# Deformable sampling on one Trainium2 core: four gather buffers, a pair of index words ahead, and three of four corners weighted by small multiply-adds

## The chip, the cores and the metric

The kernel runs on one core of one Trainium2 chip, in float32 throughout. The metric is the device time of one execution in microseconds (us); lower is better. The chip's engines are named as the profile names them: PE (TensorE, matmuls), DVE (VectorE), ACT (ScalarE), POOL (GpSimd) and SP (SyncE, which here only issues loads).

## The reference

`x` is (8, 256, 128, 128). Layer 0 normalizes it by groups, predicts offsets and a modulation with a 3x3 convolution, samples a 1x1-convolved `v` bilinearly at the offset positions, and adds a 1x1 convolution of the result to `x`. Layer 1 is a group-wise ZCA whitening of the whole batch.

```python
x = x + _L0_conv_ref(_gn(x), ...)      # per image, layer 0
    offsets = conv2d(x, offset_w, offset_b, 1)          # 2*4 channels
    mod = 1.0 + jnp.tanh(conv2d(x, mod_w, mod_b, 1))    # 4 channels
    v = conv2d(x, kv_w, kv_b, 0)[:, C:].reshape(B, HEADS, HD, H, W)
    # _sample_one: four corners of each position
    return g(x0, y0, w00) + g(x1, y0, w01) + g(x0, y1, w10) + g(x1, y1, w11)
    sampled = _sample(v, grid) * mod
    out = conv2d(sampled.reshape(B, C, H, W), out_w, out_b, 0)
x = x + _L1_conv_ref(_gn(x), ...)      # needs the covariance over all images
```

The sampling is what the change touches: for every pixel and each of 4 channel groups, 4 corners of 64 channels are fetched and summed with 4 weights (modulation folded in).

## The kernel before, in words

**Stages.** The program first takes the statistics of image 0, then runs a software pipeline over images: while image g is sampled (its `v` gathered from DRAM), image a = g + 1 goes through the convolution that makes its `v` and its offsets, and image s = g + 2 gives its statistics. Image g = 7 is sampled alone, and image 6 without a third one beside it. After the last image the whitening matrices are computed, and a last phase (L1074, L780) streams all data once through a 128x128 map.

**Tiling.** An image is 16 pairs of two blocks of 4 rows. Index `i` is the pair, `j` the block in it. For one block, POOL issues 16 indirect DMAs (`gather`, L829), one for each of 4 rows x 4 groups; each brings, for 128 pixels (partitions), a patch of 256 floats, the four corners of 64 channels. `NJ` = 16, and the half `h` holds 8 of them. So a pair has 32 gathers and 4 halves.

**Order on each engine.** Every engine runs its own program in order, with semaphores between them. For one block (i, j) in the pipeline's middle:
- DVE: `sample` of half 0 (wait for its gathers; L568 multiplies all corners by their weights, L570 and L573 add them up into `samp`), `residual` (L582) of the block before, `conv_out` (L483, L486) of rows 0 and 1 of image a, `sample` of half 1, `take_stats` (L418), `conv_out` of rows 2 and 3, and after j = 1 `place` (L510 to L555), which makes indices and weights of a pair of image a.
- PE: convolution rows 0, 1 (L929), `out_conv` of the block before (L965), `turn_x1` of it (L979, needs `residual`), row 2, after j = 1 `offsets` (L941), `turn_samples` of half 0 (L954), row 3, `turn_samples` of half 1, and `gram_block` (L994) of the block before.
- ACT: store and copy-out of the block before (`x1_store` L1116, `x1_out` L1126, needs `turn_x1`), `dup` of rows 0, 1 (L1092, L1094, needs `conv_out`), `samples_out` (L1109, needs `turn_samples` of half 1), `indices` (L1140, the index words of block (i + 1, j)), `dup` of rows 2, 3, `v_store` (L1100), and after j = 1 the tanh of the modulation (L1145).
- POOL: `gather`, which waits until `sample` of (i - 1, j) has read the patch buffer, and for the index words.
- SP: loads of x for the three images.

There are two patch buffers, one for each j. The pair loop (`pairs`, L227) runs pair 0 apart, pairs 1 to 14 in a hardware loop with one pair in its body, and pair 15 apart; for the six middle images a loop over images (L222) stands around it. At the last pair of an image DVE, PE and ACT also run `prep`, the normalization of the next image's weights (L444 to L467).

Of the kernel before, what the change touches and what calls it, by code (L numbers as in the profile page):

```python
# [5 lines left out]
ALU = mybir.AluOpType  # L25
# [27 lines left out]
NH = NJ // 2  # L53
S0 = 4 * BP
# [25 lines left out]
def deform_zca_kernel(nc, B, x, wA, biasA, bias_off, wO, bias_o, w_z, bias_z, out):  # L80
# [10 lines left out]
    with ctx:  # L91
# [28 lines left out]
        taps = sb("taps", [P, H + 2, NT])  # L120
# [3 lines left out]
        xa = [sb(f"xa{j}", [P, CC, BP]) for j in range(2)]  # L124
        vring = [sb(f"vring{j}", [P, ROWS, G, 2, CG]) for j in range(2)]
        carry = [sb(f"carry{j}", [P, G, CG]) for j in range(2)]
        index_now = [sb(f"index_now{j}", [P, NJ], U32) for j in range(2)]
        patch = [sb(f"patch{j}", [P, NJ, PATCH]) for j in range(2)]
# [7 lines left out]
        xs = [sb(f"xs{j}", [P, CC, BP]) for j in range(2)]  # L136
# [6 lines left out]
        pm = {n: sb("p_" + n, [P, QR, G]) for n in ("tm", "th", "w0", "w1", "ia")}  # L143

# [33 lines left out]
        got = [[sem(f"got{j}{h}") for h in range(2)] for j in range(2)]  # L178
        weighted = sem("weighted")
        halved = sem("halved")  # L180
# [65 lines left out]
        def offsets_use(b, q, more):  # L246


            if ends(q)[1]:
# [5 lines left out]
               for j in range(2)]  # L255
# [31 lines left out]
        y_mem = taps[:, :, :].rearrange("p r n -> p (r n)")  # L287
        y_buf = [area(y_mem, n * CC * YB, CC * YB).rearrange("p (c n) -> p c n", c=CC)
                 for n in range(NY - 2)]
# [16 lines left out]
        def _(eng):  # L306
# [9 lines left out]
            def load_s(b, i, j):  # L316

                at = eng.snap((i * 2 + j) * BP)
                p = eng.snap((b - 1) * PAIRS + i)
                eng.wait_ge(st_used[j], p + 1)  # L320
                alone(eng)
                eng.dma_start(xs[j][:, :, :], x_v[bass.ds(b, 1), :, :, bass.ds(at, BP)]
                              .rearrange("a p c n -> (a p) c n")).then_inc(st_ld[j], 16)

            def load_a(b, i, j):
# [5 lines left out]
                eng.dma_start(xa[j][:, :, :], x_v[bass.ds(b, 1), :, :, bass.ds(at, BP)]  # L331
# [13 lines left out]
            def image(g, a, s):  # L345
# [10 lines left out]
                def pair(i):  # L356
# [40 lines left out]
        def _(eng):  # L397
            for row in (0, H + 1):
                eng.memset(taps[:, row, :], 0.0).then_inc(setup_v, 1)
# [7 lines left out]
            eng.wait_ge(setup_v, 6)  # L407
# [5 lines left out]
            eng.wait_ge(setup_v, 8)  # L413
# [57 lines left out]
            def conv_out(b, i, j, rows, wide):  # L471

                for r in rows:
                    k = r % 2
# [3 lines left out]
                    if r == ROWS - 1:  # L478
# [7 lines left out]
                    eng.tensor_tensor(taps[:, bass.ds((i * 2 + j) * ROWS + r + 1, 1), :]  # L486
                                      .rearrange("p a n -> p (a n)"),
                                      bank[:, C:NA], biasB[:, C:NA], ALU.add)\
# [72 lines left out]
            def sample(b, i, j, h):  # L561

                eng.wait_ge(got[j][h], (b * PAIRS + i) * (NH * 16) + NH * 16)
                mine = patch[j][:, h * NH:(h + 1) * NH, :]
                v4 = mine.rearrange("p t (k e) -> p (t k) e", e=CG)
                w4 = weight[:, bass.ds(((i * 2 + j) * 2 + h) * (NH * 4), NH * 4)].unsqueeze(2)\
                    .to_broadcast([P, NH * 4, CG])
                eng.tensor_tensor(v4, v4, w4, ALU.mult).then_inc(weighted, 1)  # L568
                eng.wait_ge(weighted, (b * PAIRS + i) * 4 + 2 * j + h + 1)
                eng.tensor_tensor(mine[:, :, 0:ENT], mine[:, :, 0:ENT], mine[:, :, ENT:PATCH],  # L570
                                  ALU.add).then_inc(halved, 1)
                eng.wait_ge(halved, (b * PAIRS + i) * 4 + 2 * j + h + 1)
                eng.tensor_tensor(samp[j][:, 2 * h:2 * h + 2, :].rearrange("p r (g e) -> p (r g) e", g=G),  # L573
# [678 lines left out]
```

## Time and profile before

| what | value |
|---|---|
| median of 3 runs | 6903.72 us (6898.48 to 6908.78) |
| span of the profiled execution | 7542.0 us (its own time; nothing is recorded outside the span) |
| PE / DVE / ACT / POOL busy | 61% / 56% / 14% / 61% |
| mean granted TensorE clock | 0.806 |
| DMA | 1612.36 MB, mean 214 GB/s |

The profiled execution is 638 us longer than the median run. Shares of busy time are means over stages: the gathers run from 289.6 to about 6806 us of the span, and the last phase from about 6906 us to the end is bound by DMA.

### The profile page before, as it was taken

To read this page: it belongs to the slowest core of one execution; us is meant where nothing else is said; L and a number is where in the kernel's file an instruction comes from. 1 tells how busy PE (TensorE), PEld (TensorE's weight loads), DVE (VectorE), ACT (ScalarE), POOL (GpSimd) and SP (SyncE) were. 2 spreads that over 40 slices of the span, in tenths; PEclk is the share of its full clock that TensorE was granted. 3 is DMA by queue.
4 is the path that set the end of the run, shared out by engine and by line. 5 is a ranking of instruction groups with operands and counts; after the bars stand their busy time and mean duration, and the time that the engine had idled before them with its cause. 6 is when DMAs were issued, how large, how long until landed. Compare 5 with 4: busy or idle time off the path is not lost.

```text
span 7542.0 us, 73500 instructions
## 1 busy us (share of the span) xinstructions
PE 4572.0 (61%) x17916; PEld 2935.6 (39%) x17916; DVE 4223.0 (56%) x8110; ACT 1067.2 (14%) x2723; POOL 4578.9 (61%) x4115
## 2 busy tenths in 40 slices
PE   5765656565566656655665656566665544446777
PEld 3443434344344433333443434343443333234322
DVE  6655656555565555555655556555555544345555
ACT  1211111111111111111111111111111111010000
POOL 0377667676767767667676677676776777770000
PEclk9877778787788878777887878787887766667999
DMA  8866657666666666666666666565565544445999
GB/s 283 275 203 212 200 185 227 195 205 201 197 206 207 209 194 208 197 193 207 202 216 196 201 206 217 188 216 186 184 195 183 187 131 136 129 129 193 421 421 412
DMA packets 1069670, 1612.36 MB, mean 214 GB/s; under 512 B 92080, under 2 KB 617008, under 8 KB 1067568
## 3 DMA queue, kind: packets, MB, share of 16 engines
q0 software_dynamic: 196608, 537.13, 22.2%
q10 hardware_dynamic: 632832, 536.91, 22.0%
q1 hardware_dynamic: 240176, 537.77, 20.7%
q14 instruction: 42, 0.34, 0.0%
q8 instruction: 12, 0.20, 0.0%
HBM read 1074.58 MB, written 536.87 MB: 214 GB/s over the span
## 4 chain that ended last, share of the span: by engine, by line
another core or an unknown queue 21%; issue 21%; PE 19%; DVE 18%; DMA 9%; POOL 5%; DVEq 3%; ACT 3%; ACTq 1%; POOLq 0%; SPq 0%
PE psA L929 6%; DVE patch L568 5%; PE psO L965 5%; POOL patch L829 5%; DMA out_dram<-vring 4%; DVE patch L570 4%; PE psG L994 3%; DMA vring<-x 3%; PE psT L954 2%; DVE xr L582 2%; DMA v<-vring 1%; DVE vring L483 1%; PE psT L979 1%; DVE bst L418 1%
## 5 line engine op out<-in xcount | busy, mean ns | idle before, releaser
L829 POOL DMA_INDIRECT patch<-v,index_now x4096 | 4572.9, 1116 | 2224.0 <-issue 1517.0
L568 DVE TENSOR_TENSOR patch<-patch,weight 128x2048 f32<-128x2048 f32 x512 | 1171.3, 2288 | 941.4 <-DMA patch<-v,index_now 553.1
L929 PE MATMUL psA<-wB,xa 128*128 128x364 f32 x3824 | 1498.5, 529 | 185.2 <-DVE taps L486 103.1
L979 PE MATMUL psT<-ident,xr 128*128 128x128 f32 x2048 | 373.8, 343 | 1712.3 <-issue 928.5
L582 DVE SCALAR_TENSOR_TENSOR xr<-psO,bo_sb,xr 128x512 f32<-128x512 f32 x512 | 375.2, 748 | 1205.9 <-remote 972.5
L979 PEld LDWEIGHTS psT<-ident,xr 128*128 128x128 f32 x2048 | 300.6, 177 | 1917.7 <-issue 1067.8
L965 PE MATMUL psO<-sampT,wO_sb 128*128 128x512 f32 x2048 | 985.3, 626 | 73.4 <-issue 42.1
L929 PEld LDWEIGHTS psA<-wB,xa 128*128 128x128 f32 x3824 | 769.6, 218 | 574.4 <-issue 208.8
L954 PE MATMUL psT<-ident,samp 128*128 128x128 f32 x2048 | 409.9, 329 | 674.2 <-DVE samp L573 440.1
L1126 ACT ACTIVATE x1T<-psT 128x512 f32<-128x512 f32 x512 | 290.0, 596 | 3629.8 <-PE psT L979 1597.1
L994 PE MATMUL psG<-x1T 128*128 128x129 f32 x4096 | 664.6, 329 | 29.8 <-issue 18.7
L994 PEld LDWEIGHTS psG<-x1T 128*128 128x128 f32 x4096 | 643.7, 246 | 30.9 <-issue 27.1
L570 DVE TENSOR_TENSOR patch<-patch 128x1024 f32<-128x1024 f32 x512 | 627.2, 1225 | 17.6
L954 PEld LDWEIGHTS psT<-ident,samp 128*128 128x128 f32 x2048 | 289.7, 170 | 877.0 <-DVE samp L573 510.9
L965 PEld LDWEIGHTS psO<-sampT,wO_sb 128*128 128x128 f32 x2048 | 410.4, 204 | 543.5 <-issue 503.1
L1109 ACT ACTIVATE sampT<-psT 128x512 f32<-128x512 f32 x512 | 283.7, 595 | 1684.3 <-remote 711.5
L483 DVE TENSOR_TENSOR vring<-psA,biasB 128x256 f32<-128x256 f32 x734 | 303.4, 413 | 185.2 <-remote 114.7
L573 DVE TENSOR_TENSOR samp<-patch 128x512 f32<-128x512 f32 x512 | 354.2, 692 | 17.6
L1094 ACT ACTIVATE vring<-vring 128x256 f32<-128x256 f32 x768 | 290.7, 412 | 54.3 <-DVE vring L483 49.1
L941 PEld LDWEIGHTS psI<-taps,shift 128*128 128x128 f32 x2304 | 279.2, 193 | 31.2 <-issue 3.2
L418 DVE BATCH_NORM_STATS2 bst<-xs 128x512 f32 (+1 forms) x448 | 285.8, 680 | 3.9 <-DMA xs<-x_dram 3.9
L483 DVE TENSOR_TENSOR carry<-psA,biasB 128x256 f32<-128x256 f32 x222 | 92.8, 418 | 341.3 <-remote 295.6
(176 smaller groups left out, 2935.5 us busy)
## 6 DMA issues: line engine op xcount, KB each, us to landing
v<-vring ACTq DMA_DIRECT2D x256, 1024.0 KB
xa<-x_dram SPq DMA_DIRECT2D x256, 512.0 KB
xr<-x_dram SPq DMA_DIRECT2D x256, 512.0 KB
x<-xr ACTq DMA_DIRECT2D x256, 512.0 KB
xs<-x_dram SPq DMA_DIRECT2D x224, 512.0 KB
taps<-x SPq DMA_DIRECT2D x96, 1024.0 KB, 13.4
out_dram<-taps ACTq DMA_DIRECT2D x96, 1024.0 KB, 18.9
patch<-v,index_now POOLq DMA_INDIRECT x4096
```

The costliest lines, as they stand in the source:

```text
L418: ins = eng.bn_stats(bst[:, c, bass.ds(i * 2 + j, 1), :] .rearrange("p a s -> p (a s)"), xs[j][:, c, :])
L483: eng.tensor_tensor(dst, bank[:, 0:C].rearrange("p (g e) -> p g e", g=G), biasB[:, 0:C].rearrange("p (g e) -> p g e", g=G), ALU.add)\
L568: eng.tensor_tensor(v4, v4, w4, ALU.mult).then_inc(weighted, 1)
L570: eng.tensor_tensor(mine[:, :, 0:ENT], mine[:, :, 0:ENT], mine[:, :, ENT:PATCH], ALU.add).then_inc(halved, 1)
L573: eng.tensor_tensor(samp[j][:, 2 * h:2 * h + 2, :].rearrange("p r (g e) -> p (r g) e", g=G), mine[:, :, 0:CG], mine[:, :, CG:ENT], ALU.add)\
L582: eng.scalar_tensor_tensor(xr[j][:, o, :], psO[o][:, :], bo_sb[:, o:o + 1], xr[j][:, o, :], ALU.add, ALU.add)\
L829: eng.indirect_dma_start(out=patch[j][:, t, :], out_offset=None, in_=v2_flat[k], in_offset=bass.IndirectOffsetOnAxis(ap=index_now[j][:, t: ...
L929: mm = eng.matmul(conv_bank[wide][r][:, 0:NA], xa[j][:, c, r * W:(r + 1) * W], wB[:, c, :], start=(c == 0), stop=(c == CC - 1))
L954: mm = eng.transpose(psT[c][:, r * W:(r + 1) * W], samp[j][:, r, c * P:(c + 1) * P], ident[:, :])
L965: mm = eng.matmul(psO[o][:, :], wO_sb[:, h, o * P:(o + 1) * P], sampT[:, h, :], start=(h == 0), stop=(h == CC - 1))
L979: mm = eng.transpose(psT[h][:, at:at + P], xr[j][:, c, row * W:(row + 1) * W], ident[:, :])
L994: mm = eng.matmul(psG[:, c * (P + 1):(c + 1) * (P + 1)], x1T[:, r, c, 0:P], x1T[:, r, c, :], start=(opens and c == 0 and r == 0), stop=(cl ...
```

## The change

It has four parts.
- **Four patch buffers** (`RING` = 4) instead of two. The pair loop now has two pairs in its body, so that pair parity `m` picks buffer `2 * m + j` by name. A gather waits for the samples of two pairs before, not one.
- **Index words a pair ahead**: ACT copies them, and now also 64 weights per block (`weight_now`), before it does anything else for the block, instead of after `samples_out`.
- **Taps in strips**: the tap rows of image a, kept for a whole image before, live in two strips of 10 rows. The rows at a strip's edge are written twice. The buffers of the last phase move to other memory.
- **The weighting**: corner 0 of each gather is scaled by ACT in place (128x64, weight read per partition), corners 1 to 3 are multiplied and added by DVE, one 128x64 instruction for each corner and gather.

```diff
-            pair(0)
-            with eng.Fori(1, PAIRS - 1) as i:
-                pair(i)
-            pair(PAIRS - 1)
+            pair(0, 0, 0)
+            with eng.Fori(0, PAIRS // 2 - 1) as h:
+                pair(eng.snap(h * 2 + 1), 1, h)
+                pair(eng.snap(h * 2 + 2), 0, eng.snap(h + 1))
+            pair(PAIRS - 1, 1, PAIRS // 2 - 1)
...
-            def sample(b, i, j, h):
-
-                eng.wait_ge(got[j][h], (b * PAIRS + i) * (NH * 16) + NH * 16)
...
-                eng.tensor_tensor(v4, v4, w4, ALU.mult).then_inc(weighted, 1)
...
+            def sample(b, i, m, j, h):
+
+                n = 2 * m + j
+                half = (b * PAIRS + i) * 4 + 2 * j + h
+                eng.wait_ge(scaled, half + 1)
+                if h == 0:
+                    eng.wait_ge(psT_free[CC - 1], (b * PAIRS + i) * 4 + 2 * j + SAMP_FREE - 3)
+                for k in (1, 2, 3):
+                    for t in range(h * NH, (h + 1) * NH):
+                        total = patch[n][:, t, 0:CG]
+                        r, at = t // G, t % G * CG
+                        last = eng.scalar_tensor_tensor(
+                            samp[j][:, r, at:at + CG] if k == 3 else total,
+                            patch[n][:, t, k * CG:(k + 1) * CG],
+                            weight_now[n][:, t * 4 + k:t * 4 + k + 1], total, ALU.mult, ALU.add)
+                    if k < 3:
+                        last.then_inc(weighted, 1)
+                        eng.wait_ge(weighted, half * 2 + k)
+                    else:
+                        last.then_inc(sampled[j][h], 1)
...
+            def scale(b, i, m, q, j, h):
+
+                n = 2 * m + j
+                eng.wait_ge(index_cp, (b * PAIRS + i) * 2 + j + 1)
+                eng.wait_ge(got[n][h], (b * (PAIRS // 2) + q) * (NH * 16) + NH * 16)
+                for t in range(h * NH, (h + 1) * NH):
+                    corner = patch[n][:, t, 0:CG]
+                    last = eng.activation(corner, corner, ACT.Copy,
+                                          scale=weight_now[n][:, t * 4:t * 4 + 1])
+                last.then_inc(scaled, 1)
...
                     for j in range(2):
+                        if not last:
+                            if g is not None:
+                                indices(g, i + 1, 1 - m, j)
+                        elif a is not None:
+                            indices(a, 0, 0, j)
                         if g is not None:
+                            scale(g, i, m, q, j, 0)
                             if j == 1:
                                 x1_store(g, i, 0)
                                 x1_out(g, i, 0)
@@ -1161,12 +1197,8 @@
                         if ca is not None and not (prepare and j == 0):
                             dup(ca, ci, j, (0, 1))
                         if g is not None:
+                            scale(g, i, m, q, j, 1)
                             samples_out(g, i, j)
-                        if not last:
-                            if g is not None:
-                                indices(g, i + 1, j)
-                        elif a is not None:
-                            indices(a, 0, j)
```

On DVE, in the pair loop, the instructions of one half and its neighbours stood like this before (`ISA` and `REGISTER_ALU` are register steps):

```order
L568 ISA
L568 TENSOR_TENSOR patch<-patch,weight 128x2048
L569 REGISTER_ALU
L570 TENSOR_TENSOR patch<-patch 128x8x128
L573 TENSOR_TENSOR samp<-patch 128x512
L418 ISA
L418 BN_STATS bst<-xs 128x6
```

And with the change, at the same place:

```order
L562 REGISTER_ALU
L569 SCALAR_TENSOR_TENSOR patch<-patch,weight_now 128x64 x8
L575 ISA
L569 SCALAR_TENSOR_TENSOR patch<-patch,weight_now 128x64 x8
L575 REGISTER_ALU
L569 SCALAR_TENSOR_TENSOR samp<-patch,weight_now 128x64 x8
L407 ISA
L407 BN_STATS bst<-xs_mem 128x6
```

Three instructions have become 24, in three rounds of 8 with a wait between the rounds.

On ACT, block j = 1 of the pair loop before, from the copy-out of the block before to the next block (`x<-xr` is `x1_store`):

```order
L1116 DMA x<-xr 128x2x512
L1123 REGISTER_ALU
L1125 REGISTER_ALU
L1126 ACTIVATE x1T<-psT 128x4x128 x2
L1090 REGISTER_ALU
L1092 ACTIVATE vring<-carry 128x4x64
L1094 ACTIVATE vring<-vring 128x4x64
L1090 REGISTER_ALU
L1094 ACTIVATE vring<-vring 128x4x64
L1108 REGISTER_ALU
L1109 ACTIVATE sampT<-psT 128x512 x2
L1140 ACTIVATE index_now<-index 128x16
```

With the change, for one block:

```order
L1159 ACTIVATE index_now<-index 128x16
L1165 ISA
L1166 ISA
L1169 ACTIVATE patch<-patch,weight_now 128x64 x8
L1131 REGISTER_ALU
L1132 ISA
L1132 DMA x<-xr 128x2x512
L1139 REGISTER_ALU
L1141 REGISTER_ALU
L1142 ACTIVATE x1T<-psT 128x4x128 x2
L1106 ISA
L1108 ACTIVATE vring<-carry 128x4x64
```

The index words have moved from behind `samples_out` to the front, and eight scalings stand ahead of `x1_store` and `x1_out`; the other eight stand between `dup` of rows 0, 1 and `samples_out`.

At the end of `place` DVE's pair loop before branches back after each pair (the last two of four stores of `weight`, then the branch):

```order
L555 ISA
L555 SCALAR_TENSOR_TENSOR weight<-p_m,p_w 128x32
L555 ISA
L555 SCALAR_TENSOR_TENSOR weight<-p_m,p_w 128x32
L557 REGISTER_ALU
L230 REGISTER_ALU
L230 COMPARE_AND_BRANCH
```

With the change the first pair of the body runs on into the second, and only the second ends with a branch back:

```order
L552 SCALAR_TENSOR_TENSOR weight<-p_m,p_w 128x32
L554 REGISTER_ALU
L562 ISA
L569 SCALAR_TENSOR_TENSOR patch<-patch,weight_now 128x64 x8
L575 ISA
```

Counted in the built programs, with register steps and waits, one pass of DVE's pair loop in the middle images has 114 instructions before and 390 after; one pass of the loop over images around it had 322 before, without repeating the pair loop. ACT's pair loop goes from 58 to 193.

## Rows read from the trace of the kernel before

**Rows 1.** Busy time by window, the gathers' stretch; its first row names the columns.

```profile
core 0: us, PE busy (x) PEld busy (x) DVE busy (x) ACT busy (x) POOL busy (x), PEclk, DMA share, GB/s
289.60:6813.00 6523.40, 3833.10 (x15847) 2566.99 (x15848) 3618.92 (x6699) 995.32 (x2535) 4572.94 (x4096) 0.78 0.61 193
```

**Rows 2.** The page, part 5, gathers: busy us, mean ns of one, idle before.

```profile
L829 POOL DMA_INDIRECT patch<-v,index_now x4096 | 4572.9, 1116 | 2224.0 <-issue 1517.0
```

**Rows 3.** Waits of POOL: us in total, times, longest us.

```profile
POOL patch L829 <- ACT index_now L1140: 707.0, 105, 15.9
```

**Rows 4.** Timeline 2999:3006, POOL and DVE: start us, us, instruction, [idle before].

```profile
3000.45 0.94 POOL L829 DMA_INDIRECT patch<-v,index_now  x1 [0.30 <-issue]
3001.49 2.29 DVE L568 TENSOR_TENSOR patch<-patch,weight 128x2048 f32<-128x2048 f32 x1 [5.03 <-DMA patch<-v,index_now]
3001.70 2.90 POOL L829 DMA_INDIRECT patch<-v,index_now  x1 [0.30 <-issue]
3003.81 1.23 DVE L570 TENSOR_TENSOR patch<-patch 128x1024 f32<-128x1024 f32 x1
```

**Rows 5.** Timeline 3140:3185, one block whose patches had all landed.

```profile
3154.84 2.29 DVE L568 TENSOR_TENSOR patch<-patch,weight 128x2048 f32<-128x2048 f32 x1 [0.78 <-DVE weight L555]
3159.03 1.40 DVE L582 SCALAR_TENSOR_TENSOR xr<-psO,bo_sb,xr 128x512 f32<-128x512 f32 x2
3161.32 1.09 ACT L1126 ACTIVATE x1T<-psT 128x512 f32<-128x512 f32 x2 [8.55 <-PE psT L979]
3162.59 0.72 ACT L1094 ACTIVATE vring<-vring 128x256 f32<-128x256 f32 x2
3165.27 0.69 DVE L573 TENSOR_TENSOR samp<-patch 128x512 f32<-128x512 f32 x1
3168.09 2.28 DVE L568 TENSOR_TENSOR patch<-patch,weight 128x2048 f32<-128x2048 f32 x1
3168.60 0.38 ACTq L1100 DMA_DIRECT2D v<-vring  x1
```

**Rows 6.** Timeline 3140:3185, `place` and small operations beside it.

```profile
3150.57 0.18 DVE L510 TENSOR_TENSOR p_tm<-psI,off_b 128x32 f32<-128x32 f32 x1
3150.98 0.22 ACT L1140 ACTIVATE index_now<-index 128x16 uint32 x1
3151.08 0.42 ACT L1094 ACTIVATE vring<-vring 128x256 f32<-128x256 f32 x1
3152.49 0.22 DVE L540 SCALAR_TENSOR_TENSOR p_m<-p_ix,p_b 128x64 f32<-128x64 f32 x1
3152.64 0.22 DVE L542 TENSOR_TENSOR p_m<-p_ix,p_c 128x64 f32<-128x64 f32 x1
```

**Rows 7.** Timeline 7010:7016, DVE in the last phase.

```profile
7011.95 1.41 DVE L780 SCALAR_TENSOR_TENSOR vring<-psT,patch,vring 128x512 f32<-128x512 f32 x2 [2.26 <-PE psG L1074]
7013.27 0.74 DVE L780 SCALAR_TENSOR_TENSOR vring<-psI,patch,vring 128x512 f32<-128x512 f32 x1
```

**Rows 8.** Timelines 3140:3185 and 3000:3056, PE's `out_conv` at two clocks.

```profile
3170.75 3.60 PE L965 MATMUL psO<-sampT,wO_sb 128*128 128x512 f32 x8
...
3038.34 6.39 PE L965 MATMUL psO<-sampT,wO_sb 128*128 128x512 f32 x8 [3.56 <-issue]
```

**Rows 9.** Timeline 1924:1977, DVE from image to image.

```profile
1926.67 2.28 DVE L568 TENSOR_TENSOR patch<-patch,weight 128x2048 f32<-128x2048 f32 x1
1950.84 2.28 DVE L568 TENSOR_TENSOR patch<-patch,weight 128x2048 f32<-128x2048 f32 x1
...
1967.55 0.52 DVE L555 SCALAR_TENSOR_TENSOR weight<-p_m,p_w 128x32 f32<-128x32 f32 x4
1969.64 0.41 DVE L591 TENSOR_TENSOR gram<-gram,psG 128x258 f32 x1
1976.07 2.29 DVE L568 TENSOR_TENSOR patch<-patch,weight 128x2048 f32<-128x2048 f32 x1 [6.01 <-issue]
```

**Rows 10.** The page, part 3, the queue of instruction packets.

```profile
q14 instruction: 42, 0.34, 0.0%
```

More of the change, by code:

```diff
@@ L134, in deform_zca_kernel @@
         gram_tail = sb("gram_tail", [P, B, CC, P + 1])
-        xs = [sb(f"xs{j}", [P, CC, BP]) for j in range(2)]
+        xs_mem = sb("xs_mem", [P, 2, CC, BP])
         bst = sb("bst", [P, CC, BLOCKS, 6])
@@ L143, in deform_zca_kernel @@
         pm = {n: sb("p_" + n, [P, QR, G]) for n in ("tm", "th", "w0", "w1", "ia")}
+        xa = [xa_mem[:, j, :, :] for j in range(2)]
+        xs = [xs_mem[:, j, :, :] for j in range(2)]
         psA = [ps(f"psA{i}") for i in range(2)]
@@ L177, in deform_zca_kernel @@
         index_cp = sem("index_cp")
-        got = [[sem(f"got{j}{h}") for h in range(2)] for j in range(2)]
+        got = [[sem(f"got{n}{h}") for h in range(2)] for n in range(RING)]
+        scaled = sem("scaled")
+        edge = sem("edge")
         weighted = sem("weighted")
-        halved = sem("halved")
         sampled = [[sem(f"sampled{j}{h}") for h in range(2)] for j in range(2)]
@@ L397, in _ @@
         def _(eng):
-            for row in (0, H + 1):
-                eng.memset(taps[:, row, :], 0.0).then_inc(setup_v, 1)
+            eng.memset(taps[:, 0, 0, :], 0.0).then_inc(setup_v, 1)
             eng.memset(x1T[:, :, :, :], 1.0).then_inc(setup_v, 1)
@@ L469, in prep, with conv_out @@
                 eng.wait_ge(psI_free, b * NU + 3)
-            def conv_out(b, i, j, rows, wide):
+            def conv_out(b, i, m, j, rows, wide):
+                top = ends(i)[0]
                 for r in rows:
-                    k = r % 2
+                    k, row = r % 2, j * ROWS + r
                     eng.wait_ge(row_full[j][r], b * PAIRS + i + 2)
@@ L610, in pair @@
                     prepare = last and ca is not None
+                    if last and a is not None and s is None:
+                        eng.memset(taps[:, m, QR + 1, :], 0.0).then_inc(edge, 1)
                     for j in range(2):
                         if g is not None:
-                            sample(g, i, j, 0)
+                            sample(g, i, m, j, 0)
                             if j == 1:
@@ L839, in _ @@
                     alone(eng)
-                    with eng.Fori(0, PAIRS) as i:
-                        for j in range(2):
-                            gather(b, k, i, j)
+                    with eng.Fori(0, PAIRS // 2) as q:
+                        for m in range(2):
+                            for j in range(2):
+                                gather(b, k, q * 2 + m, m, j)
         def whiten_tensor(eng):
@@ L931, in conv_rows, with offsets @@
                     mm.then_inc(row_full[j][r], 1)
-            def offsets(b, q, more):
+            def offsets(b, q, m, more):
+                bottom = ends(q)[1] and not more
                 for k in range(2):
-                    eng.wait_ge(psA_free[k], (b * PAIRS + q) * 4 + 5 + (0 if ends(q)[1] else 2))
+                    eng.wait_ge(psA_free[k], (b * PAIRS + q) * 4 + (5 if bottom else 7))
+                if bottom:
+                    eng.wait_ge(edge, 1)
                 eng.wait_ge(psI_free, offsets_use(b, q, more))
```

115 lines of the change are left out of this document (63 added, 52 removed).

## The prediction

> **What bounds the kernel now.** I read the windows first. The gathers fill 6523 us of the 7542 us span [rows 1]; what lies around them, 1019 us, is statistics, the first convolution, the whitening and a DMA-bound last phase, which the change leaves alone but for the places of some buffers. The gathers are 4096 = 128 pairs of 32, and they last 1116 ns in the mean with about 0.30 us between two [rows 2, 4]. So POOL needs 32 x (1.116 + 0.305) = 45.5 us for a pair. The profiled execution spends 51 us on a pair, but it is 638 us longer than the median run. If the 1019 us are the same in both, an undisturbed run spends (6904 - 1019) / 128 = 45.98 us on a pair: within half a microsecond of what POOL needs with no wait at all. In an undisturbed run POOL is the bound, and its waits for the index words (707 us in the profile, [rows 3]) have mostly gone. I therefore work in time per pair and apply the difference to the median.
>
> Second, why a gather takes 1.116. Undisturbed it takes 0.94; the one that starts at 3001.70 takes 2.90, and ends 0.82 us after DVE's 2.29 us multiply L568 [rows 4]. It waits until the big two-input instruction is over, and then it gets through although L570, again with two inputs, has already begun. There are four L568 a pair, and (1.116 - 0.949) x 32 = 5.3 us a pair is their price. 0.949 is what I take for a free gather, from 0.94 to 0.95 in the timelines.
>
> Third, how fast the other engines could go. At 3154.84 all patches had landed, and the next block's first L568 follows 13.25 us later [rows 5]. With the 4.3 us of `place` in every second block [rows 6] that is about 31 us a pair, far under POOL's 45.5. DVE, PE and ACT are waiting for POOL now.
>
> **POOL after the change.** No instruction of 2.29 us is left in the gathers' way. If the small ones hand over between two of them, as L568 does to the gather ahead of L570 [rows 4], each gather loses at most part of one small instruction, and POOL needs 32 x (0.949 + 0.305) = 40.1, say 40.5 us. If DVE kept POOL out through all 24, POOL would need about 48; the handover row speaks against it. Buffers and early index words remove waits of which, by the sum above, an undisturbed run has half a microsecond a pair. So POOL offers 5.5 us a pair. Whether they are taken depends on the others.
>
> **One DVE multiply-add, d.** A 64-column two-input instruction without a pointer starts 0.15 us before the next [rows 6]; that is the low end. The weight here is read per partition. L780 is such an instruction: two take 1.41 us and one 0.74, so the second starts 0.67 after the first [rows 7]. A column costs (2.29 - 1.23) / 1024 = 1.035 ns [rows 4], 0.53 for 512, so 0.14 is fixed; with 64 columns d = 0.20. The high end is no overlap at all, 0.74 - 0.53 + 0.07 = 0.28. I take 0.20, the nearest row. A half becomes 24d + 0.3 (two waits between rounds, and the tail) = 5.1 us, where before L568 to the end of `sample` is 2.32 + 1.26 + 0.69 = 4.2.
>
> **One ACT scaling, a.** No row shows an activation with a pointer. Without one, 16 columns are followed after 0.10 us [rows 6] and 256 after 0.31 (the pair in 0.72, [rows 5]): 0.14 for 64 columns, the low end. Without overlap 0.22 + 48 x 0.0009 = 0.26, the high end. DVE's pointer costs 0.05 (0.15 to 0.20), which would give 0.19; I take 0.23, between that and the high end. Eight take 8a + 0.1 = 1.9 us, and DVE can't begin before the last one is done.
>
> The Trainium skill, ScalarE: Activation LUTs, section What ACT_TABLE_LOAD costs, gives 186 ns + 0.833 ns a column, 93 ns for each pointer operand, and 93 ns of overlap. By it a would be 0.24 (an estimate from that page), and the sum below 25 to 30 us higher; no run here has shown it yet.
>
> **The chain of a block.** With POOL out of the way the in-order chain is what sets the time, and ACT now stands in it. From the block of [rows 5]:
> - scalings of half 0, 8a + 0.1; its sample, 24d + 0.3; `residual`, 1.4.
> - from its end (3160.43) PE turns x1, ACT copies it out and does `dup` of rows 0, 1, until 3163.31: 2.9 us, of which the next ACT instruction can take back 0.1. Before, `sample` of half 1 went on beside this. Now its scalings are queued behind it.
> - scalings of half 1, 8a + 0.1; its sample, 24d + 0.3.
> - from its end (3165.96) to the issue of the v store (3168.98) ACT has 3.0 us, then 0.25 of index and weight words, before the next block's scalings.
>
> Sum for j = 0: 16a + 48d + 8.25. After j = 1 DVE has `take_stats` and rows 2, 3 (2.4 us with the doubled tap row) and then `place`, 4.3 us from 3150.57 to 3154.84; the scalings hide behind them: 8a + 48d + 11.5. A pair is 24a + 96d + 19.75 = 5.5 + 19.2 + 19.75 = 44.5 us. It was 31 before; it is now over POOL's 40.5.
>
> PE adds a little. From the end of `sample` of half 1 (3165.96) PE reaches the end of `out_conv` at 3174.35, 8.4 us, with the clock at its upper level [rows 5, 8]; the next `residual` needs it after 3.25 + 1.9 + 5.1 = 10.3 us. At the lower level `out_conv` alone takes 6.4 instead of 3.6 [rows 8], and is late by 0.9. The granted clock is 0.78 in this stretch [rows 1], and PE now idles longer inside a block. I add 0.5 us a pair, bounds 0 and 1.2.
>
> **The loop body.** In the loop over images DVE's way back, over 322 instructions, costs it a stop: the last store of `weight` ends at 1968.07, and the next image's first L568 starts at 1976.07, with only `residual` and `gram_add` in between and 6.01 us idle on "issue" [rows 9]. At the pair loop's way back (114 instructions) the same place takes 0.78 us [rows 5]. The difference is an instruction fetch, about 6.8 us. The changed pair loop has 390 instructions on DVE, more than the 322 that had to be fetched again. So I expect the stop at each of the 7 passes an image: 6.8 x 7 / 16 = 3.0 us a pair. It falls right behind `place`, where the chain runs on DVE. Bounds: nothing if the body stays resident, twice that if a second stop comes.
>
> The Trainium skill, Runtime: NRT & Kernel Launch, section Instruction fetch mechanics, says that a taken branch to a page that isn't in the current window of two forces a fetch and a stall; the 6.01 us of [rows 9] agrees. It also puts 512 instructions into that memory, by which 390 fit if they lie in two pages; then this term is nothing, which is the first rival below.
>
> **Image ends.** With POOL waiting anyway, `prep` was hidden. From the L568 at 1926.67 to the one at 1950.84 is 24.2 us [rows 9], where two halves take 13.25 [rows 5]; of the 17.6 more I count 14, since PE has less behind it afterwards, six times.
>
> **Sum.** Images 0 to 5: 16 x (44.5 + 0.5 + 3.0) + 14 = 782 each, 4692. Image 6, without statistics, 1.2 less a pair: 749. Image 7 has no convolution, `dup` or `place`; its chain is about 39, under POOL: 16 x 40.5 = 648. Together 6089, against 128 x 45.98 = 5885: 204 us more, 6904 + 204 = 7108, which I round to **7105 us**. DMA moves the same bytes at a share of 0.61 [rows 1] and isn't a bound at 48 us a pair.
>
> **Rivals.**
> - *The loop stays resident.* Then 48 us go in each of seven images: 6775. For it: the ratio of 390 to 322 says little if pages' edges decide.
> - *POOL stays the bound.* With d = 0.14 and a = 0.14 the chain is 36.6, and with the stop 39.6: POOL sets 40.5, the time is 6904 - 128 x 5.5 = 6200. It needs the pointer to cost nothing on either engine; L780 speaks against it. The chain decides from 40.5 us on, which is d = 0.12 with the stop and a = 0.23.
> - *Small instructions don't overlap on DVE* (d = 0.28): 7.7 us more in 112 pairs and 6 in the last 16, 8065. L780's overlap of 0.07 speaks against it.
> - *The stop comes twice a pass*: 7105 + 7 x 48 = 7440.
> - *Costs cancel*: the chain at 45.98 with a short stop; nothing measurable, within 0.2%, 14 us, which is what a measurement of this kernel tells from no change.
>
> **How the numbers follow.** My forecast 0.53, resident loop 0.20, POOL 0.10, twice 0.07, no overlap 0.05, cancel 0.05. The likeliest case's own range is 6950 to 7280: d by 0.01 is 110 us, a by 0.03 80, the clock 80. To leave out no more than 2 in 10 the range goes from 6700, below the resident loop's 6775, to 7350. Faster: POOL 0.10, most of the resident loop 0.17, a corner of the forecast 0.03: 0.30. Same 0.05. Slower 0.65.
>
> **What the changed profile would show.** Gathers of more than 1 us nearly gone, and POOL waiting for index words or samples instead; DVE's 128x64 instructions 0.20 us apart, ACT's 0.23; DVE idle in front of half 1's first multiply-add until ACT's scaling; an idle of some 6 us on "issue" behind every second `place`, and several hundred instruction packets where there are 42 now [rows 10]. I am wrong if pairs run at 40 us with POOL never waiting, or if the packets stay few.

## The result, and the profile after

| | median | runs |
|---|---|---|
| before | 6901.1 us | 6886.09 to 6908.78, 4 |
| changed | 7044.98 us | 7034.64 to 7056.14, 4 |

The ratio is 1.0209, 95% interval 1.0194 to 1.0223: the change makes the kernel 2.1% slower. The forecast was 7105. The profiled execution of the changed kernel took 7052.57 us, its span is 7050.8, so its stretches can be read against the median directly.

From the page, changed kernel: busy time, the instruction queue, the chain that ended last, and three groups (busy us, mean ns, idle before):

```profile
PE 4741.2 (67%) x17916; PEld 3135.5 (44%) x17916; DVE 4642.1 (66%) x19126; ACT 2116.8 (30%) x7075; POOL 3934.5 (56%) x4115
...
q14 instruction: 302, 2.47, 0.1%
...
DVE 45%; ACT 19%; issue 14%; PE 9%; DMA 8%; ACTq 2%; DVEq 1%; SPq 0%
...
L838 POOL DMA_INDIRECT patch<-v,index_now x4096 | 3928.6, 959 | 2366.6 <-issue 1557.5
L569 DVE SCALAR_TENSOR_TENSOR patch<-patch,weight_now 128x64 f32<-128x64 f32 x8192 | 1701.3, 280 | 1838.2 <-ACT patch L1169 1530.8
...
L1169 ACT ACTIVATE patch<-patch,weight_now 128x64 f32<-128x64 f32 x4096 | 1030.0, 336 | 0.5
```

The gathers are nearly free now, 959 ns where [rows 2] has 1116, and they keep POOL busy 644 us less (3928.6 against 4572.9). The chain that ended last holds no POOL: it is DVE and ACT, and DVE waits 1531 us for ACT's scaling.

The timeline of two blocks, DVE (a pair starts at 2977.39, the next at 3022.63, its second block at 3044.45):

```profile
2970.45 0.60 DVE L552 SCALAR_TENSOR_TENSOR weight<-p_m,p_w 128x32 f32 x4
2977.39 1.26 DVE L569 SCALAR_TENSOR_TENSOR patch<-patch,weight_now 128x64 f32<-128x64 f32 x6 [6.34 <-issue]
...
3022.63 3.35 DVE L569 SCALAR_TENSOR_TENSOR patch<-patch,weight_now 128x64 f32<-128x64 f32 x16 [0.34 <-DVE weight L552]
3026.01 1.66 DVE L569 SCALAR_TENSOR_TENSOR samp<-patch,weight_now 128x64 f32<-128x64 f32 x8
3027.58 1.41 DVE L584 SCALAR_TENSOR_TENSOR xr<-psO,bo_sb,xr 128x512 f32<-128x512 f32 x2
...
3033.86 3.35 DVE L569 SCALAR_TENSOR_TENSOR patch<-patch,weight_now 128x64 f32<-128x64 f32 x16 [3.36 <-ACT patch L1169]
3037.25 1.66 DVE L569 SCALAR_TENSOR_TENSOR samp<-patch,weight_now 128x64 f32<-128x64 f32 x8
...
3044.45 3.35 DVE L569 SCALAR_TENSOR_TENSOR patch<-patch,weight_now 128x64 f32<-128x64 f32 x16 [3.35 <-ACT patch L1169]
...
3073.51 1.67 DVE L569 SCALAR_TENSOR_TENSOR patch<-patch,weight_now 128x64 f32<-128x64 f32 x8 [7.15 <-issue]
```

And ACT in the first of them:

```profile
3029.93 1.08 ACT L1142 ACTIVATE x1T<-psT 128x512 f32<-128x512 f32 x2 [7.85 <-PE psT L992]
3030.90 0.42 ACT L1108 ACTIVATE vring<-carry 128x256 f32<-128x256 f32 x1
3031.21 0.72 ACT L1110 ACTIVATE vring<-vring 128x256 f32<-128x256 f32 x2
3031.82 2.01 ACT L1169 ACTIVATE patch<-patch,weight_now 128x64 f32<-128x64 f32 x8
```

Two things can be read from these rows. Half 1 can't start at 3030.5, when DVE is through with rows 0 and 1, but waits 3.36 us: its scalings are queued on ACT behind x1's copy-out, which waits for PE, which waits for `residual`. And the pair that begins behind the loop's way back (2970.45 to 2977.39, 3067 to 3073.51) has 6.3 and 7.2 us idle on "issue", where the same place inside the body (3022.63) has 0.34. Over all 42 such ways back the idle time before the pair is 4.8 to 7.6 us, 6.6 in the median.

Measured from the first L569 of a pair to the next, a pair takes 45.2 us without the way back and 50.5 with it (medians of images 0 to 5); an image 771 to 776 us, of which the last pair has 65 to 69; image 6 732; a pair of image 7 39.5. In image 7 POOL gathers nearly without a pause, a pair in 40.6, yet it doesn't hold DVE up: from its second pair on DVE reaches a half 11 to 26 us after the half's last gather, and waits there for nothing but ACT's scalings. It works off a stock of patches at its own pace.

### The profile page after: what moved, and what is told of

It reads as the page before. It is cut to its first block, busy times and chain, and to the rows that moved or that the text cites. A ratio compares the mean times of both kernels' runs of the same rounds, so it can differ in the third digit from the quotient of the medians.

```text
span 7050.8 us, 87497 instructions
## 1 busy us (share of the span) xinstructions
PE 4741.2 (67%) x17916; PEld 3135.5 (44%) x17916; DVE 4642.1 (66%) x19126; ACT 2116.8 (30%) x7075; POOL 3934.5 (56%) x4115
## 3 DMA queue, kind: packets, MB, share of 16 engines
q10 hardware_dynamic: 632832, 536.91, 22.5%
## 4 chain that ended last, share of the span: by engine, by line
DVE 45%; ACT 19%; issue 14%; PE 9%; DMA 8%; ACTq 2%; DVEq 1%; SPq 0%
DVE patch L569 22%; ACT patch L1169 11%; DVE samp L569 10%; DMA out_dram<-vring 4%; DVE xr L584 3%; ACT vring L1110 3%; PE psT L992 3%; DMA vring<-x 3%; DVE bst L407 2%; PE psT L967 1%; ACT x1T L1142 1%; DMA v<-vring 1%; ACT sampT L1125 1%; ACT vring L1108 1%; PE psA L939 1%
## 5 line engine op out<-in xcount | busy, mean ns | idle before, releaser
L838 POOL DMA_INDIRECT patch<-v,index_now x4096 | 3928.6, 959 | 2366.6 <-issue 1557.5
L569 DVE SCALAR_TENSOR_TENSOR patch<-patch,weight_now 128x64 f32<-128x64 f32 x8192 | 1701.3, 280 | 1838.2 <-ACT patch L1169 1530.8
L939 PE MATMUL psA<-wB,xa_mem 128*128 128x364 f32 x3824 | 1502.6, 533 | 93.5 <-DVE taps L485 86.8
L1169 ACT ACTIVATE patch<-patch,weight_now 128x64 f32<-128x64 f32 x4096 | 1030.0, 336 | 0.5
L939 PEld LDWEIGHTS psA<-wB,xa_mem 128*128 128x128 f32 x3824 | 799.4, 226 | 482.8 <-issue 136.3
L569 DVE SCALAR_TENSOR_TENSOR samp<-patch,weight_now 128x64 f32<-128x64 f32 x4096 | 849.6, 280 | 18.2
L1007 PE MATMUL psG<-x1T 128*128 128x129 f32 x4096 | 855.6, 396 | 7.7 <-ACT x1T L1142 7.7
L1007 PEld LDWEIGHTS psG<-x1T 128*128 128x128 f32 x4096 | 835.3, 311 | 9.5 <-issue 7.1
L407 DVE BATCH_NORM_STATS2 bst<-xs_mem 128x512 f32 (+1 forms) x448 | 285.9, 681 | 3.9 <-DMA xs_mem<-x_dram 3.9
L954 PE MATMUL psI<-taps,shift 128*128 128x96 f32 x2304 | 279.6, 277 | 0.0
```

What stands on the lines that cost most here:

```text
L407: ins = eng.bn_stats(bst[:, c, bass.ds(i * 2 + j, 1), :] .rearrange("p a s -> p (a s)"), xs[j][:, c, :])
L569: last = eng.scalar_tensor_tensor(samp[j][:, r, at:at + CG] if k == 3 else total, patch[n][:, t, k * CG:(k + 1) * CG], weight_now[n][:, t ...
L838: eng.indirect_dma_start(out=patch[n][:, t, :], out_offset=None, in_=v2_flat[k], in_offset=bass.IndirectOffsetOnAxis(ap=index_now[n][:, t: ...
L939: mm = eng.matmul(conv_bank[wide][r][:, 0:NA], xa[j][:, c, r * W:(r + 1) * W], wB[:, c, :], start=(c == 0), stop=(c == CC - 1))
L954: mm = eng.matmul(psI[:, 0:QR * NO].rearrange("p (r o) -> p r o", o=NO), shift[:, dx, :], taps[:, m, dy:dy + QR, t * NO:(t + 1) * NO], sta ...
L1007: mm = eng.matmul(psG[:, c * (P + 1):(c + 1) * (P + 1)], x1T[:, r, c, 0:P], x1T[:, r, c, :], start=(opens and c == 0 and r == 0), stop=(cl ...
```

## The experiments

**First, a thing that most of them met.** In four of the six sets of runs below the kernel before took 7471 to 7635 us, not 6900. Their traces show why: a semaphore update often arrives microseconds after the instruction that makes it. Timeline of the changed kernel in a run of that kind (after_again), PE and DVE:

```profile
3029.19 1.39 PE L939 MATMUL psA<-wB,xa_mem 128*128 128x364 f32 x4
3031.11 1.66 DVE L569 SCALAR_TENSOR_TENSOR samp<-patch,weight_now 128x64 f32<-128x64 f32 x8
3032.68 0.42 DVE L473 TENSOR_TENSOR vring<-psA,biasB 128x256 f32<-128x256 f32 x1
...
3036.49 1.11 PE L967 MATMUL psT<-ident,samp 128*128 128x128 f32 x4 [5.91 <-remote]
...
3038.22 0.42 DVE L473 TENSOR_TENSOR carry<-psA,biasB 128x256 f32<-128x256 f32 x1 [4.95 <-remote]
```

The sample that PE turns at 3036.49 was finished at 3032.77, and the row that DVE takes at 3038.22 had left PE at 3030.6; the semaphore events that end these two waits stand at 3036.45 and 3038.11. Counted from the semaphore events of each trace, the table gives the share of PE's, DVE's and ACT's updates that came over 0.3 us late, for those made while POOL gathers (a burst is the 16 gathers of a block) and for all others:

```
trace           while POOL gathers  else    mean gather us  burst of 16 us  between bursts us
changed kernel  0.001               0.000   0.959           19.9            2.1
before          0.348               0.020   1.116           22.5            0.3
r_big           0.347               0.016   1.113           22.3            0.3
b_piece4        0.448               0.018   0.984           20.3            4.4
r_piece4        0.482               0.025   0.980           20.3            6.3
b_new2          0.467               0.029   0.958           19.9            10.2
after_again     0.558               0.030   0.960           20.0            7.1
a_straight      0.566               0.038   0.960           19.9            7.0
a_pace          0.002               0.000   0.966           22.1            1.1
a_fs_again      0.003               0.000   0.962           20.0            0.3
```

The shares are soft. The traces with late updates record only 69 to 80% of the updates of PE, DVE and ACT, and 12 to 24% of those of the gathers, where the others record 98% or more. With every update that finds no record counted as late, the share is 0.49 for before and 0.65 for after_again; with those left out that find none within 15 us, 0.35 and 0.54. It stays under 0.005 for the changed kernel, a_pace and a_fs_again either way. The time is no matter of counting: with late updates the kernel before takes 8 to 11% longer, the changed kernel 17%.

So the trace of before, from which I predicted, was one with late updates, and its time (7542 us) lies among those of the kernel before in the late sets; that accounts for the 638 us over its median. It is no trait of one chip: after_again (late) and a_fs_again (prompt) ran on the same one. I call the runs late and prompt; each ratio is to the kernel before, run beside it on the same chip.

**r_big** (late): the changed kernel with the old weighting.

```diff
-                        last = eng.scalar_tensor_tensor(   # 24 a half
...
+                            last = eng.tensor_tensor(v4, v4, w4, ALU.mult)   # 128x2048, then two additions
...
-                            scale(g, i, m, q, j, 0)   # and half 1: nothing is scaled on ACT
```

> The changed kernel (four patch buffers, index words a pair ahead, taps in strips, pair loop of two pairs) with the old weighting: three wide DVE instructions a half, nothing scaled on ACT. Theory A (the new weighting's chain through ACT and DVE costs the time, and POOL was the bound before): gathers are held back again, mean 1.10 to 1.12 us, POOL 45.5 us a pair with hardly a wait, so 128 x 45.5 + 1050 = 6870, within 0.5% of before; the loop body of some 300 DVE instructions may still stop at its way back, but POOL has buffers ahead and hides it. Theory B (the four-buffer structure with its long loop body is what slows the kernel): 7000 or more, with DVE's stops on the chain. Rival C (before, POOL really lost more to late index words than half a microsecond a pair): 6750 or less.

Measured: 1.0145 (1.003 to 1.0259; it rests on two runs, 7522 and 7541 us, since the other two took 7649 and 14676). Gathers:

```profile
L847 POOL DMA_INDIRECT patch<-v,index_now x4096 | 4556.8, 1113 | 2219.5 <-issue 1551.6
```

The slow gathers are back, as theory A has it, and bursts follow each other after 0.3 us. With late updates B is out: the structure costs 1.5% here, not 10 like the whole change (after_again). No run has this kernel with prompt updates, so the 6870 of A and the 6750 of C stay untested.

**b_new, b_new2** (late, on two chips): the new weighting alone in the kernel before.

```diff
+scale(g, i, j, 0)   # ACT, ahead of x1_store / x1_out
+scale(g, i, j, 1)   # ACT, ahead of samples_out
```

> The kernel before (two buffers, loop of one pair, index words after the block) with the new weighting alone: corner 0 on ACT, 24 multiply-adds a half on DVE. Theory A: the chain of a pair is 45.2 us, as between two stops in the changed kernel, but the loop of some 210 DVE instructions stays resident and has no stop: images 0 to 5 are 16 x 45.2 + 21 = 744, image 6 713, image 7 about 660, with 1020 around them 6860: 0 to 1% faster than before, some 180 faster than the changed kernel. Theory B (the new weighting in itself costs the 2%, whatever the loop): 7040 or more. If two buffers make POOL late as well, pairs are at 47 or more, POOL idle on index words, and 7100 or more.

> The same kernel as b_new (the new weighting alone in the kernel before). Its loop over pairs, 201 instructions on DVE, came back in 0.3 us each time in b_new. Where updates are prompt, theory A expects pairs at 45 to 46 us, no stop, 6860 with bounds 6800 and 6960; theory B (the new weighting costs the 2% whatever the loop) 7040 or more; if two buffers make POOL late, 7100 or more. If updates are late again, as b_new, 15% over the kernel before.

Measured: 1.1499 (1.1421 to 1.1577) and 1.1763 (1.1681 to 1.1845). The way back of the pair loop (201 instructions) took DVE 0.2 to 0.5 us every time. My time was missed by far; POOL was idle 7.4 (b_new) and 10.2 us (b_new2) between bursts in the median, in all 2423 and 2638 us for index words. That with two buffers late signals also stop POOL fits this, but wasn't tested by itself. What the weighting costs alone with prompt updates stays open.

**b_piece4** (late): the old weighting in pieces of 512 columns.

```diff
-eng.tensor_tensor(v4, v4, w4, ALU.mult)                 # 128x2048
+for q0 in range(0, NH, NH // parts): ... eng.tensor_tensor(...)   # parts 4, 2, 1; all 128x512
```

> The kernel before with its wide weighting cut into pieces of 512 columns: four multiplies, two additions, one addition a half, all on DVE, nothing else changed. Theory A (a gather waits for the end of the one DVE instruction with two inputs that it meets, so its length is the price): gathers of 2.9 us are gone, none loses more than about 0.6, the mean falls from 1.116 to about 1.0, POOL needs 41 to 42 us a pair; two buffers and late index words may leave it waiting a little; 6330 to 6550. Rival (DVE keeps POOL out for its whole two-input work, however it is cut): mean stays at 1.10 or more, time within 1% of before or slower, since the pieces add some 0.3 us a half.

Measured: 1.0116 (1.0053 to 1.0178); gathers

```profile
L841 POOL DMA_INDIRECT patch<-v,index_now x4096 | 4029.6, 984 | 2805.1 <-issue 1529.0
```

The mechanism of [rows 4] is confirmed: the same columns in shorter instructions take 132 of the 167 ns off a gather. The 543 us that POOL saves went into the pauses between bursts, 4.4 us in the median instead of 0.3. **r_piece4** (late), the same in the changed kernel:

> The changed kernel (four buffers, early index words, loop of two pairs, 258 instructions on DVE) with the weighting in wide pieces on DVE and nothing on ACT: four multiplies, two additions, one addition of 512 columns a half. It takes both costs away at once: no 2.29 us instruction ahead of POOL, no ACT link and no stop at the way back (226 instructions came back in 0.3 to 0.7 in r_big). Gathers at a mean of 0.98 as in b_piece4. Where updates are prompt, theory A: POOL needs 32 x (0.98 + 0.305) = 41.1 us a pair, DVE's chain 32 to 34, so 128 x 41.1 + 1050 = 6310, bounds 6250 and 6450. Rival (something else than POOL and the ACT link set the pairs): 6800 or more. Where updates are late, POOL's burst of 20.5 us and what follows it stand in a row: 51 us a pair, 7450 to 7600, about the kernel before.

Measured 1.057 (1.0502 to 1.0637), above the range that I gave for late updates: 6.3 us between bursts.

**a_actfirst, a_first2** (late, two chips): ACT's order.

```diff
 scale(g, i, m, q, j, 0)
+scale(g, i, m, q, j, 1)
 x1_store(...); x1_out(...); dup(...)
-scale(g, i, m, q, j, 1)
 samples_out(g, i, j)
```

> The changed kernel with ACT's order changed in one place: the eight scalings of half 1 follow those of half 0 at once, ahead of x1_store, x1_out and dup. Theory A (half 1 waits 3.3 us a block because its scalings are queued behind x1_out and dup): DVE's idle before the half-1 multiply-adds goes from 3.3 to 3.8 us to nearly 0, a pair from 45.2 to about 39, then POOL's 39.5 to 40.5 is the bound; the stops stay but are mostly covered by patches fetched ahead; 6300 to 6450. Rival (PE is right behind ACT: the idle only moves to residual, which waits for out_conv): pairs at 43 or more, 6800 to 7000. Rival (the scalings take a share of something DVE needs): DVE's multiply-adds get longer than 0.20 apart.

> The same kernel as a_actfirst (all sixteen scalings of a block ahead of ACT's other work), run again because in the four runs so far a third of the semaphore updates came microseconds after the instruction that made them, where in the changed kernel's trace all but 7 come within 0.02 us, and the kernel before took 7471 us beside them, not 6901. Where updates are prompt, theory A expects DVE's wait ahead of half 1 gone, pairs at 39 to 41 us with POOL as the bound, 6300 to 6450. Rival (the idle moves to PE's out_conv and turns): pairs at 43 or more, 6800 or more. If updates are late again, the run is as a_actfirst, about 9% over the kernel before.

Measured: 1.0923 (1.0857 to 1.0989) and 1.0918 (1.0846 to 1.0991). DVE's idle ahead of half 1 went from 3.8 us (after_again) to nothing in the median, as expected, and the time hardly moved: pairs still alternate between 60 and 50 us as in after_again below, and DVE is idle 189 us an image until an update that the trace puts down to "remote", where after_again has 74 (means of images 1 to 5).

**a_straight and after_again** (late, side by side): DVE's program written out.

```diff
+if eng is nc.vector:
+    for i in range(PAIRS):
+        pair(i, i % 2, i // 2)
+    return
 pair(0, 0, 0)
 with eng.Fori(0, PAIRS // 2 - 1) as h:
```

> The changed kernel with DVE's program alone written out for all 16 pairs of an image instead of a loop of two pairs; every other engine keeps its loop, and no operation is added or left out. Theory A (the way back over 390, or 370, instructions stops DVE for 5 to 6 us, six times in each of seven images, and nothing covers it): every pair of images 0 to 5 takes 45.2 us, the 50.5 us pairs are gone, 42 x 5.3 = 220 us less where updates are prompt: 6825, 1.1% under the kernel before. Straight code has no taken branch, so instructions arrive ahead. Rival (the 5.3 us are no fetch but work at the seam of the loop, or code that runs straight is fetched as late): pairs alternate 45.2 and 50.5 as before, 7045. If updates are late again the idle after place goes too, but less of the time, since late updates set the pairs.

> The changed kernel itself, beside the kernel before on this chip. If updates are prompt: ratio 1.021 as before. If they are late: theory A (each signal between ACT, DVE and PE costs more there, and the changed kernel has more of them in a row in a block) 1.08 to 1.12, pairs at 53 to 60 us; rival (late updates cost both kernels the same time) 1.02.

Measured: a_straight 1.0928 (1.0866 to 1.0991), the changed kernel 1.0997 (1.0936 to 1.1058). Pairs of image 0 are, in us:

```
after_again  53.8 54.2 60.0 49.8 59.9 49.3 60.0 49.8 60.1 50.5 60.1 50.4 60.2 51.2 54.3 72.3
a_straight   53.4 54.2 54.8 54.1 54.8 53.3 54.8 54.1 54.8 53.4 54.8 53.6 54.1 53.4 54.2 72.6
```

The 60 and 50 (a stop, and the pair after it catching up) become 54: the stop belongs to the taken branch; between the pairs of straight code it is gone, though instructions are fetched there too (221 packets against 303). a_fs_again below shows it with prompt updates: between its pairs DVE has no idle time on "issue" at all. The loop over images still branches back, over 2929 instructions, and there DVE still stops, 2.7 to 5.0 us here and 4.9 to 6.2 in a_fs_again. The intervals of the two ratios overlap; by one trace of each, an image of 0 to 5 takes 887.0 instead of 899.5 us in the mean, 2.1 us a stop, since the next pair catches up with most of it where updates are late.

**a_pace** (prompt): POOL slowed down.

```diff
     ).then_inc(got[n][t // NH], 16)
+    eng.memset(idle[:, t, :], 0.0).then_inc(paced, 1)      # 128x192, after every gather
```

> The changed kernel with a small write of POOL's own (192 columns of a scratch tile) behind every gather, and nothing else changed: POOL gathers more slowly, a gather every 1.5 to 1.6 us instead of 1.25. Theory L (where updates are late, the chip hands on only some 11 of them a microsecond; every gather makes 16, so 16 in a burst of 20 us are 12.8 a microsecond, a backlog builds up behind which the signals of PE, DVE and ACT wait, and it has gone some 3 us after the burst; the kernel before, whose gathers DVE holds up, makes 11.3): at 10 to 10.7 a microsecond there is no backlog, the share of updates that are late while POOL gathers falls from 0.56 to under 0.2, the 7 us between two bursts shrink to 1 or less, a pair is 49 to 52 us instead of 54 to 55: 7450 to 7750, that is 0.99 to 1.03 of the kernel before instead of 1.10, though POOL does more. Rival (updates are late whenever POOL gathers, at any pace): share still 0.5, bursts of 24.5 and 7 between them, 63 us a pair, 9000. Where updates are prompt: POOL at 49 to 51 becomes the bound, 7350 to 7550.

Measured: 7174.46 us, 1.0391 (1.0374 to 1.0408). Timeline, POOL:

```profile
5899.40 0.95 POOL L842 DMA_INDIRECT patch<-v,index_now  x1 [0.17 <-issue]
5900.35 0.27 POOL L846 MEMSET idle<- 128x192 f32 x1
5900.79 0.95 POOL L842 DMA_INDIRECT patch<-v,index_now  x1 [0.17 <-issue]
```

A gather every 1.39 us, not my 1.5 to 1.6, so 7350 was too high. It ran with prompt updates, so theory L (a limit of some 11 updates a microsecond) is untested. But it is the cleanest test of what bounds the changed kernel. POOL now needs 46.4 us a pair instead of 40.6. A pair of image 7 goes from 39.5 to 46.2 us, 87 us over 15 pairs: there POOL has become the bound, and DVE reaches a half 4 to 5 us after its last gather. An image of 0 to 5 goes from 772.7 to 778.8 in the mean, 0.4 us a pair, though POOL needs 5.8 more: there it isn't the bound.

**a_first_straight** (late) and **a_fs_again** (prompt): the same kernel twice, ACT's order and DVE's straight code together.

> The changed kernel with ACT's sixteen scalings at the start of the block and DVE's program written out, both edits of the runs before together. Where updates are prompt, theory A: chain 45.2 - 6.7 = 38.5 us a pair and no stop, POOL's 39.5 to 40.5 sets the pairs, 6200 to 6300, 10% under the kernel before. Rival (PE's out_conv or the turns take the idle's place): 6600 or more. Where updates are late, DVE's waits come from the updates that the burst of gathers holds back, and the two edits take 0.6% each or less: 8080 to 8170, 8 to 9% over the kernel before.

> The same kernel as a_first_straight (scalings of both halves at the start of the block, DVE's program written out), run again since the chips differ and one with prompt updates can tell the theories apart by time. Where updates are prompt, theory A: chain 45.2 - 6.7 = 38.5 us a pair and no stop, POOL's 39.5 to 40.5 sets the pairs; 128 x 40.2 + 6 x 10 for the ends of images + 1050 = 6250, bounds 6150 and 6450, some 9% under the kernel before. Rival (PE's out_conv or the turns take the place of the idle time): pairs at 43 or more, 6600 or more. Where updates are late, as a_first_straight: 1.06 to 1.09 of the kernel before, pairs at 54.

Measured: late 1.0688 (1.0641 to 1.0735). Prompt: **6226.34 us** (6222.82 to 6239.29) against 6917.1, ratio 0.8999 (0.8986 to 0.9011), where 6250 was expected. From its page, the chain and the gathers, and DVE in one block:

```profile
q14 instruction: 221, 1.81, 0.1%
...
POOL 50%; issue 19%; DMA 10%; DVE 8%; PE 8%; ACT 3%; ACTq 1%; POOLq 0%; DVEq 0%; SPq 0%
...
L842 POOL DMA_INDIRECT patch<-v,index_now x4096 | 3940.8, 962 | 1546.3 <-issue 1538.6
```

```profile
3001.00 3.36 DVE L573 SCALAR_TENSOR_TENSOR patch<-patch,weight_now 128x64 f32<-128x64 f32 x16 [3.36 <-ACT patch L1173]
3004.40 1.66 DVE L573 SCALAR_TENSOR_TENSOR samp<-patch,weight_now 128x64 f32<-128x64 f32 x8
3005.97 1.41 DVE L588 SCALAR_TENSOR_TENSOR xr<-psO,bo_sb,xr 128x512 f32<-128x512 f32 x2
...
3008.30 3.39 DVE L573 SCALAR_TENSOR_TENSOR patch<-patch,weight_now 128x64 f32<-128x64 f32 x16
3011.73 1.66 DVE L573 SCALAR_TENSOR_TENSOR samp<-patch,weight_now 128x64 f32<-128x64 f32 x8
```

Half 1 starts 7.30 us after half 0 instead of 11.23, with no wait. POOL now waits for nothing: its 1546.3 us before gathers are 4095 times 0.305 and the 297 before the first one, against 2366.6 in the changed kernel; DVE reaches a half 4 us after its last gather in image 7, so here POOL is the bound. Images 0 to 5 take 652 us in the mean instead of 773, image 6 632 instead of 732. The same operations and bytes, 12% less time than the changed kernel.

## Why the prediction was right

Slower was right, by 144 us instead of 204. By its steps:

- **POOL before and after.** The price of L568 is confirmed by r_big (1113 ns) and b_piece4 (984); the gathers came to 959 instead of 949, and a POOL that hardly waits needs 40.4 to 40.6 us a pair (a_fs_again, and image 7 of the changed kernel), forecast 40.1 to 40.5. That the kernel before was bound by POOL with prompt updates rests on the arithmetic from its median; no prompt trace of it was taken, so it is argued, not shown.
- **d and a.** From start to start, DVE's multiply-adds lie 0.20 us apart (eight in 1.66, the last one 0.28; a half takes 5.04, forecast 5.1), forecast 0.20. ACT's eight in 2.01 with 0.336 for the last give a = 0.239, forecast 0.23. The prices that the Trainium skill gives in ScalarE: Activation LUTs, section What ACT_TABLE_LOAD costs (186 ns + 0.833 a column, 93 for a pointer operand, 93 of overlap), come to an estimate of 0.24 for it, and the trace agrees.
- **The chain of a block.** Forecast 44.5 + 0.5 us (the terms for j = 1 add to 11.6, not 11.5), measured 45.2. The wait where it was said to be: 3.36 us in front of half 1, for scalings queued behind `x1_out` and `dup`. With the order changed it is gone: in a_fs_again the row of half 1 (3008.30) has no wait.
- **The stop.** Forecast 6.8 us at seven passes, measured 5.3 (a pair of 50.5 against 45.2) at six: a loop of seven passes has six ways back. The 6.8 doesn't follow from [rows 9] and [rows 5]: there the idle time is 6.01 at the image's way back against 0.78 at the pair loop's, so the stop was worth 5.2 (5.5 with 0.24 more ahead of `residual`), which is what was measured. So 42 stops, 215 us (36 x 5.3 and six of 4.0 in image 6), where I had 336. It was the largest miss in size, and both of its factors were too high. "Several hundred packets" came as 302.
- **Image ends.** Forecast 14 us more than a pair, measured 21.5 in the mean.
- **Image 7.** 39.5 a pair, forecast 40.5 with POOL as the bound. DVE's chain set the pace, which the prediction had at about 39: it took the slower of the two for the bound and left out that DVE starts the image with a stock of patches, on which it can run faster than POOL. a_pace, where a half is used 4 to 5 us after its gathers, shows what POOL as the bound looks like.
- **Around the gathers**, which I left as they were, 26 us came on top: 16 before the first one and 10 after the last; their cause is open.
- An image of 0 to 5: forecast 782, measured 773. The difference is 16 less for the stops (6 x 5.3 against 48) and 8 more for the end.

So the mechanism was right, and that the sum is off by only some 60 us is in part luck: the stops were 121 us too many in all, the ends of images (45) and what lies around the gathers (26) too few, while image 7 was put some 20 too long.

Of the rivals, "POOL stays the bound" at 6200 was wrong for this change and nearly right for a_fs_again (6226), as it had to be: it is what POOL offers once nothing else is in the way. The resident loop is excluded by the stops. The two edits of a_fs_again weren't run apart with prompt updates; from the changed kernel's trace the stops hold about 215 of the 819 us, and the rest would be ACT's order. That is a subtraction and not a measurement, and since POOL becomes the bound at 40.5 us a pair, the two shares needn't add up. Nor were the four buffers or the new weighting run alone with prompt updates.

## What to carry to other kernels

When a change frees the engine that bounds a kernel, write down the in-order chain of every other engine for one unit of work, with the new instructions at their place in each queue: here eight small scalings cost 3.4 to 3.8 us a block because of what stood ahead of them, and moving them, with DVE's loop written out, turned 2.1% slower into 10.0% faster without touching an operation. Count the instructions of an unrolled loop body before trusting it to come back for free: here 258 did and 390 didn't. Before trusting a profile whose own time is far over the median, look whether its waits name an instruction or only "remote".

## What the runs showed of the hardware

- **Way back of a loop on DVE.** Behind the way back of pair loops of 114 to 258 instructions DVE's next instruction came within 0.8 us. 370 and 390 stopped DVE for 4.3 to 7.0 us, with five packets of 8192 bytes fetched a pass, in the 390 loop the first 4.2 us behind the branch in the median. Every loop over images stopped DVE a few instructions behind its branch, by no rule of size: 322 instructions (before) 5.8 to 6.0 us, some 460 (r_big) 1.4 to 2.0, 590 (b_new) 4.4 to 5.5, 788 (changed) 2.3 to 3.4, 2929 (a_fs_again) 4.9 to 6.2. ACT came back over some 350 instructions (before) in 0.2 us and over some 780 (changed) in 2.5. The Trainium skill, Runtime: NRT & Kernel Launch, section Instruction fetch mechanics, says that a taken branch out of the current two-page window stalls, which it gives as a reason for unrolling in full; the stops and a_straight agree. It puts that memory at 512 instructions. Why 322 and 390 don't stay on DVE and some 350 do on ACT, no run here shows.
- **Late semaphore updates.** In the late runs 35 to 57% of the updates made while POOL was gathering came late by the table's count, and 2 to 4% of the others. After bursts of 20 us they crowd 2 to 3 us behind the last gather. An estimate from that: a burst makes 256 updates (16 a gather: the changed kernel's trace records 65268 for 4096), and 256 in 20 + 2.7 us are about 11 a microsecond. A path that hands on no more would explain why every kernel that frees POOL loses there, but that is argued, not shown: the bursts of 22.5 us show no such group, and the run meant to test it met prompt updates. What switches a chip between the two isn't known.
- With late updates the changed kernel is 10.0% slower than before, not 2.1%, and a_first_straight 6.9% slower where it is 10.0% faster with prompt ones. The sign of a change can hang on it.
